# A fused attention and MLP kernel: in the first batch, each projection unit for the second batch computed in two halves, one in each of two steps, with Q's scale one step later and K's three

## The chip, the cores and the metric

The kernel runs on one core of one Trainium2 chip. The metric is the device time of one execution in microseconds (us). A run gives one such time; the profile below is of one more execution of the same program.

## What is computed

The input is 8 sequences of 1024 positions with 256 channels. An attention layer with 16 heads of 16 channels is followed by a layer norm, a three-layer MLP with weights of +1 and -1, and a second layer norm. The part of the reference that the change touches is the projection to q, k and v and what is done to it:

```python
qkv = (x @ w_qkv.T + b_qkv).reshape(b, n, 3, H, D).transpose(2, 0, 3, 1, 4)
q, k, v = (qkv[0], qkv[1], qkv[2])
q = jax.nn.elu(q) + 1.0
k = jax.nn.elu(k) + 1.0
q = _apply_rope(q, sin, cos)
k = _apply_rope(k, sin, cos)
attn = jnp.einsum('bhnd,bhmd->bhnm', q, k) * scale
attn = jax.nn.softmax(attn, axis=-1)
attn_out = jnp.einsum('bhnm,bhmd->bhnd', attn, v)
...
return attn_out + lepe
```

The MLP is `x @ w` three times with `relu(h) * 2` between, and each layer norm is taken over the sum of its input and the layer's result.

## The kernel before

**Steps.** A sequence is a batch, b. Its 16 heads are worked in 8 pairs (n counts pairs over all batches), and a pair in 8 steps, one for each tile kt of 128 keys: 64 steps a batch (`BATCH`), 512 in all. In step s, TensorE (PE) computes four "S" units, the scores of step s + 12 with queries on partitions, from which VectorE (DVE) takes a row maximum (`row_max`, L931), and four "T" units, the scores of step s with keys on partitions, on which ScalarE (ACT) takes the exponential (`exp_probs`, L763). S and T matmuls use different halves of the array and are issued in pairs (L559, L569). PE then multiplies the exponentials of step s - 1 with v (`weighted_v`, L604, "PV" below). A step's two halves are `scores_both(s, 0)` and `scores_both(s, 1)`.

**Units and the table.** All other matmul work is cut into units of one PSUM bank each, and a table written out by hand, `dealt()`, gives each a step. In batch 0 these are, for batch c = 1: four Q units and four K units ("proj", L631; two 128x512 float32 matmuls, one for each half of the 256 input channels, `kc`), four V units (L642, four 128x256 float32 matmuls), and two "scale" units (L587, L588) that sum the relu totals over heads. Two further kinds have fixed places: "O rows" (L619) in step kt = 2 and "max rows" (L612) in step kt = 5. In a step with dealt units PE's order is: `scores_both(s, 0)`, own units, dealt units, `scores_both(s, 1)`, then both halves of PV together. Without dealt units PV's first half stands between the two score blocks. `pieces_of` cuts a unit in two pieces, which the table puts into steps that follow each other; before, only MLP units L1 and L2 (from batch 1 on) are cut.

**Banks.** In batch 0 S units use banks 0, 1 and 4, T units banks 2 and 3, and all the others take banks 5 and 6 in turn. A unit takes its bank at its first piece (`wait_free`: the unit before it in this bank must have been read) and holds it until its reader is done.

**Readers.** In order, on ACT, step s does: two exponentials, the ELU of the Q or K unit whose last piece was the last dealt piece of step s - 1 (`elu_inputs`, L799 and L800), in kt = 2 the copy of O rows (L776), in some steps `copy_v` (L784), two exponentials, in kt = 0 `copy_o` (L769), and in steps 8 to 27 one piece of the MLP weights' conversion (`weights`, L831 or L835). DVE in step s does two row maxima, the V unit or scale of step s - 1 (`v_out`, L1012; `make_scale`), the max rows, `join_sums` (L967: it adds the relu totals, and the scale unit on PE waits for it by `sums_joined`), and two row maxima. GpSimd (POOL) takes the ELU's results on: `elu`, `rotate_side`, `split`, and a DMA to scratch in DRAM, from which SyncE's queue (SP) loads the stacks of pair 8 and later.

**Places in batch 0, before.** Q units in steps 6 to 9, `join_sums` for them in 11, their scale in 14; K units in 22 to 25, `join_sums` in 27, scale in 28; V units in 46 to 49. Later batches have their own table entries.

Of the kernel before, what the change touches and what calls it, by code (L numbers as in the profile page):

```python
# [34 lines left out]
NB, N, C = 8, 1024, 256  # L35
# [3 lines left out]
KC = C // P  # L39
# [25 lines left out]
O_ROWS_STEP, RECIPROCAL_STEP, MAX_ROWS_STEP = 2, 3, 5  # L65

Q_AT = 6
V_AT = {1: (46, 47, 48, 49)}
K_AT, SCALE_AT = {1: 22}, ({}, {1: 28})
STATS_AT = {**{6 + t // 2: (0, t) for t in range(0, T, 2)}, 27: (1, 4), 29: (1, 6), 59: (1, 0), 61: (1, 2)}  # L70
MOMENTS_AT = {10: 0, 31: 1}
NORMALISE_AT = ({13: 0, 14: 2, 15: 4, 16: 6}, {37 + t: t for t in range(T)})
# [4 lines left out]
def k_at(c):  # L77
    return K_AT.get(c, 32)


def v_at(c):
    return V_AT.get(c, (46, 51, 52, 53))

# [4 lines left out]

def pieces_of(unit):

    return [(unit, part) for part in range(2 if unit[0] in ("L1", "L2") else 1)]


def proj_units(c, which):
# [204 lines left out]
def build(nc, x, xT, wT, b_qk, b_v, w_lepe, b_lepe, cos, sin, k0, k1, k2, s0, s1, s2, out):  # L299
    with ExitStack() as ctx:  # L300
# [3 lines left out]
        def sem(name):  # L304
            return ctx.enter_context(nc.semaphore(name))
# [81 lines left out]
        w_kv_loaded = sem("w_kv_loaded")  # L387
# [6 lines left out]
        xT_loaded = sem("xT_loaded")  # L394
# [30 lines left out]
        units = Units(unit_banks, unit_full, unit_free)  # L425
# [127 lines left out]
        def _(pe):  # L553
# [26 lines left out]
            def head_bounds(unit):  # L580

                _, c, w = unit
                pe.wait_ge(dve_setup, 3)
                pe.wait_ge(sums_joined, 2 * c + w + 1)
                units.wait_free(pe, unit)
                bank, total = units.out(unit), sums[:, w:w + 1]
                nc.tensor.matmul(bank[:, 0:1], same_head[:], total, start=True, stop=True, skip_group_check=True)  # L587
                nc.tensor.matmul(bank[:, 1:1 + H], total.to_broadcast([P, P]), head_mask[:], start=True, stop=True,  # L588
                                 skip_group_check=True).then_inc(units.full_sem(unit), 1)
# [30 lines left out]
                                               o_sb[:, blk * P:(blk + 1) * P], ident[:])  # L620
                done.then_inc(units.full_sem(unit), 1)

            def project(unit):

                _, c, ct, half = unit
                pe.wait_ge(xT_loaded, (c + 1) * 16)
                if c == 0 and ct == 2 and half == 0:
                    pe.wait_ge(w_kv_loaded, 16)
                units.wait_free(pe, unit)
                for kc in range(KC):  # L630
                    done = nc.tensor.matmul(units.out(unit), wT_sb[:, kc, ct * P:(ct + 1) * P],  # L631
                                            xT_sb[:, kc, half * 512:(half + 1) * 512],
                                            start=kc == 0, stop=kc == KC - 1)
                done.then_inc(units.full_sem(unit), 1)

            def project_v(unit):
                _, c, i = unit
                units.wait_free(pe, unit)
                for t in range(2):
                    for kc in range(KC):  # L640
                        col = (2 * i + t) * P
                        done = nc.tensor.matmul(units.out(unit)[:, t * C:(t + 1) * C], xT_sb[:, kc, col:col + P],  # L642
                                                wT_sb[:, kc, 2 * C:3 * C], start=kc == 0, stop=kc == KC - 1)
                done.then_inc(units.full_sem(unit), 1)

            def transpose_h(unit):
                _, m, th, kc = unit
                if m == TAIL and th == 1:
                    pe.wait_ge(tail_done[0], T // 2)
                else:  # L650
                    pe.wait_ge(ln_done[0], m * T + T // 2 * (th + 1))
                units.wait_free(pe, unit)
                for t in range(4):
                    done = nc.tensor.transpose(units.out(unit)[:, t * P:(t + 1) * P],
                                               rows_of(m)[:, 4 * th + t, kc * P:(kc + 1) * P], ident[:])
                done.then_inc(units.full_sem(unit), 1)
# [35 lines left out]

            def dense(unit, part):
                if unit[0] == "proj":
                    project(unit)
                elif unit[0] == "V":
                    project_v(unit)
                elif unit[0] == "scale":
                    head_bounds(unit)
                elif unit[0] == "hT":  # L700
                    transpose_h(unit)
                elif unit[0] == "L2":
                    ffn_out(unit, part)
                else:
                    hidden(unit, part)
# [214 lines left out]
        def _(dve):  # L920
# [7 lines left out]
            def row_max(v, h, half):  # L928
                unit, t = ("S", v, h, half), v % T
                units.wait_full(dve, unit)  # L930
                nc.vector.reduce_max(maxima[:, v // T % 2, h * T + t, half:half + 1], units.out(unit), AXIS_X)\  # L931
                  .then_inc(units.free_sem(unit), 1)
# [185 lines left out]
            for s in range(STEPS):  # L1118
                n, kt = divmod(s, T)
                b, i = s // BATCH, s % BATCH  # L1120
                v = s + T + LEAD
                if v < STEPS:
                    for half in range(2):
                        row_max(v, 0, half)
                for unit in done_behind(s - 1):
                    dense(unit)
                for unit in own_units(s):
                    if unit[0] == "max rows":
                        split_max_rows(unit[1])
                for w, at in enumerate((Q_AT, k_at(b + 1))):  # L1130
                    if b + 1 < NB and i == at + 5:
                        join_sums(b + 1, w)
                if kt == RECIPROCAL_STEP and n > 0:
                    reciprocal_o(n - 1)
                for unit in done_within(s):
                    dense(unit)
                if i in STATS_AT:
                    which, t = STATS_AT[i]
                    m = b - 2 if which == 1 and t >= T // 2 else b - 1
                    if m >= 0:  # L1140
                        if which == 0 and t == 0:
                            dve.wait_ge(sum_ready, m + 1)
                        if which == 1:
                            units.wait_read(dve, ("L2", m, t // (T // 2), t % (T // 2) // 2))
                        for tile in (t, t + 1):
                            ln_stats_of(m, which, tile)
                if i in MOMENTS_AT:
                    which = MOMENTS_AT[i]
                    m = b - 1 - which
                    if m >= 0:  # L1150
                        ln_moments(m, which)
                if v < STEPS:
                    for half in range(2):
                        row_max(v, 1, half)
                    if v % T == T - 1:
                        join_maxima(v // T)
# [37 lines left out]
            for unit in END_UNITS[len(LATE_UNITS):]:  # L1194
# [6 lines left out]
                if unit[:3] == ("L2", m, 1):  # L1201
                    t = T // 2 + 2 * unit[3]
# [208 lines left out]
```

## Time and profile before

| | |
|---|---|
| median of 3 runs | 2185.26 us |
| the 3 runs | 2184.11, 2188.7, 2185.26 us |
| profiled execution, its own time | 2188.8 us |
| its span | 2187.0 us |
| mean granted TensorE clock | 0.982 of full |
| PE busy | 2104.7 us, 96% of the span |
| DVE busy | 1673.0 us, 76% |
| ACT busy | 1491.6 us, 68% |
| POOL busy | 916.1 us, 42% |

Busy time of PE is rough, since ends of matmuls are modelled: the starts of its instructions tell more than its busy share. Batch 0 runs from step 0 at 86.80 us to step 64 at 286.77 us of the span. Steps are found in the trace by counting ACT's exponentials (L763), four a step; a step's time below is that of its first exponential. Step 6 begins at 105.71 us, step 16 at 141.26, step 22 at 159.18, step 32 at 195.22, step 46 at 232.81, step 55 at 262.13. The time from the first exponential of a step to that of the next, before, is:

| steps | us each |
|---|---|
| 6 to 15 | 4.26, 3.99, 4.87, 3.85, 4.33, 2.92, 2.90, 2.75, 2.91, 2.78 |
| 22 to 31 | 3.85, 3.99, 4.54, 3.66, 4.14, 3.07, 4.77, 2.81, 2.73, 2.48 |
| 46 to 54 | 4.27, 4.00, 4.17, 3.83, 2.80, 2.49, 2.48, 2.69, 2.58 |

### The profile page before, as it was taken

How to read it: one execution, taken by the hardware profiler on the slowest of the kernel's cores; microseconds unless marked ns; L12 is line 12 of the kernel's file. 1: busy time of each engine (PE TensorE's matmuls, PEld its weight loads, DVE VectorE, ACT ScalarE, POOL GpSimd, SP SyncE). 2: the span in 40 equal slices, each digit the busy share in tenths (PEclk: the TensorE clock that was granted, in tenths of full speed). 3: DMA queues.
4: the chain of work that ended last, by engine and by line, in shares of the span. 5: the costliest groups of instructions: out<-in, count | busy, mean ns of one | idle time of the engine just before them, and what ended most of it. 6: DMA issues, size and time to landing. Idle time of an engine off the chain costs nothing.

```text
span 2187.0 us, 43073 instructions
## 1 busy us (share of the span) xinstructions
PE 2104.7 (96%) x16896; PEld 850.9 (39%) x16896; DVE 1673.0 (76%) x3027; ACT 1491.6 (68%) x2867; POOL 916.1 (42%) x530
## 2 busy tenths in 40 slices
PE   4999999999999999999999999999999999999988
PEld 2133333344433434334343443434343343434345
DVE  7888888787787887778787877878778788877233
ACT  3298788766767667776777767776677766767532
POOL 2548159430856037470484407661275704300000
PEclk8599999999999999999999999999999999999999
DMA  5101110011010200111000110002101110000001
GB/s 179 31 14 41 54 37 26 25 49 38 16 35 18 87 17 9 35 55 54 14 25 25 66 40 16 28 16 75 31 15 35 31 56 16 16 9 28 2 0 39
DMA packets 40428, 76.85 MB, mean 35 GB/s; under 512 B 15025, under 2 KB 19489, under 8 KB 37281
## 3 DMA queue, kind: packets, MB, share of 16 engines
q1 hardware_dynamic: 35040, 51.02, 8.5%
q0 software_dynamic: 5184, 23.07, 2.8%
q8 instruction: 134, 2.20, 0.4%
q14 instruction: 70, 0.57, 0.1%
HBM read 46.27 MB, written 25.17 MB: 33 GB/s over the span
## 4 chain that ended last, share of the span: by engine, by line
PE 83%; DVE 10%; ACT 4%; issue 1%; DMA 1%; SPq 0%; POOL 0%; POOLq 0%; DVEq 0%; ACTq 0%
PE unit_banks L674 25%; PE unit_banks L559 22%; PE o_bank L604 20%; DVE maxima L931 6%; PE unit_banks L687 5%; PE unit_banks L631 5%; ACT probs L763 3%; PE unit_banks L642 2%; PE unit_banks L569 2%; PE unit_banks L619 1%; DVE hT L1000 1%; DVE h0T L1003 1%; PE unit_banks L612 0%; ACT h0T L822 0%; DMA xT_sb<-in_xT 0%
## 5 line engine op out<-in xcount | busy, mean ns | idle before, releaser
L931 DVE TENSOR_REDUCE maxima<-unit_banks 128x1 f32<-128x512 f32 x2048 | 1308.2, 684 | 367.9 <-PE unit_banks L559 364.1
L763 ACT ACTIVATE probs<-unit_banks 128x512 f32<-128x512 f32 x2048 | 1115.9, 597 | 565.6 <-PE unit_banks L569 559.9
L559 PE MATMUL unit_banks<-k_stack,q_stack 48*128 48x512 f16 x2048 | 655.1, 391 | 44.1 <-DMA k_stack<-k_scratch 23.4
L569 PE MATMUL unit_banks<-q_stack,k_stack 50*128 50x512 f16 x2048 | 648.9, 386 | 4.7 <-ACT probs L763 3.5
L604 PE MATMUL o_bank<-probs,v_pair 128*32 128x256 f32 x8192 | 565.5, 388 | 0.6
L674 PE MATMUL unit_banks<-h0T,w 128*128 128x512 f16 x2048 | 480.2, 380 | 0.0
L1258 POOL TENSOR_TENSOR attn<-o_rows_sb,rden 128x256 f32<-128x256 f32 x63 | 39.2, 622 | 875.8 <-DVE rden L944 864.7
L559 PEld LDWEIGHTS unit_banks<-k_stack,q_stack 48*128 48x128 f16 x2048 | 154.8, 94 | 562.8 <-DVE maxima L931 277.1
L604 PEld LDWEIGHTS o_bank<-probs,v_pair 128*32 128x32 f32 x8192 | 207.4, 109 | 297.6 <-issue 217.9
L674 PEld LDWEIGHTS unit_banks<-h0T,w 128*128 128x128 f16 x2048 | 188.9, 98 | 223.9 <-issue 34.2
L569 PEld LDWEIGHTS unit_banks<-q_stack,k_stack 50*128 50x128 f16 x2048 | 155.2, 93 | 36.2 <-ACT probs L763 27.7
L1003 DVE SCALAR_TENSOR_TENSOR h1T<-unit_banks,h1T 128x512 f16<-128x512 f32 x128 | 87.3, 682 | 79.9 <-ACT h1T L822 79.8
L1274 POOL TENSOR_TENSOR lepe_tmp<-v_ext,lepe_rows 128x1024 f32<-128x1024 f32 x48 | 113.1, 2357 | 70.3 <-DVE max_rows L952 67.7
L631 PE MATMUL unit_banks<-xT_sb,wT_sb 128*128 128x512 f32 x256 | 126.5, 622 | 9.8 <-DMA xT_sb<-in_xT 9.8
L674 PE MATMUL unit_banks<-hT,w 128*128 128x512 f16 x512 | 124.4, 386 | 3.5 <-DVE hT L1000 2.2
L687 PE MATMUL unit_banks<-w,h1T 128*128 128x256 f16 x1024 | 123.2, 275 | 2.7 <-DVE h1T L1003 2.7
L1276 POOL TENSOR_TENSOR rows<-rows,lepe_tmp 128x1024 f32<-128x1024 f32 x48 | 113.2, 2359 | 3.8
L822 ACT ACTIVATE h1T<-unit_banks 128x512 f16<-128x512 f32 x128 | 77.1, 602 | 49.3 <-PE unit_banks L674 49.3
L1290 POOL TENSOR_TENSOR neg_mean<-moments,ln_consts 128x8 f32<-128x8 f32 (+2 forms) x18 | 3.8, 210 | 251.7 <-DVE moments L1042 251.7
L687 PEld LDWEIGHTS unit_banks<-w,h1T 128*128 128x128 f16 x1024 | 97.2, 99 | 25.4 <-issue 10.4
L1003 DVE SCALAR_TENSOR_TENSOR h0T<-unit_banks,h0T 128x512 f16<-128x512 f32 x128 | 87.6, 686 | 18.7 <-ACT h0T L822 18.5
L822 ACT ACTIVATE h0T<-unit_banks 128x512 f16<-128x512 f32 x128 | 77.5, 605 | 16.3 <-PE unit_banks L674 13.1
(126 smaller groups left out, 1556.7 us busy)
## 6 DMA issues: line engine op xcount, KB each, us to landing
rows<-in_x POOLq DMA_DIRECT2D x8, 1024.0 KB, 5.2
xT_sb<-in_xT SPq DMA_DIRECT2D x8, 1024.0 KB, 14.2
q_stack<-q_scratch SPq DMA_DIRECT2D x128, 64.0 KB, 2.1
k_stack<-k_scratch SPq DMA_DIRECT2D x128, 64.0 KB, 2.0
q_scratch<-parts POOLq DMA_DIRECT2D x14, 512.0 KB, 3.3
k_scratch<-parts POOLq DMA_DIRECT2D x14, 512.0 KB, 3.3
out<-rows SPq DMA_DIRECT2D x7, 1024.0 KB, 4.0
q_stack<-q_scratch SPq DMA_DIRECT2D x128, 32.0 KB, 1.9
```

What stands on the lines that cost most here:

```text
L559: nc.tensor.matmul(units.out(unit), q_stack[row:row + STACK, r, t * P:(t + 1) * P], k_stack[row:row + STACK, r, half * 512:(half + 1) * 51 ...
L569: nc.tensor.matmul(units.out(unit), k_stack[row:end, r, kt * P:(kt + 1) * P], q_stack[row:end, r, half * 512:(half + 1) * 512], start=True ...
L604: done = nc.tensor.matmul(o, v_pair[:, n % RING, kt, h, :], p[:, :, parity, :], start=kt == 0 and half == 0, stop=kt == T - 1, skip_group_ ...
L631: done = nc.tensor.matmul(units.out(unit), wT_sb[:, kc, ct * P:(ct + 1) * P], xT_sb[:, kc, half * 512:(half + 1) * 512], start=kc == 0, st ...
L674: done = nc.tensor.matmul(units.out(unit), w, a, start=k == 0 and i == 0, stop=k == tiles - 1 and i == 1)
L687: done = nc.tensor.matmul(units.out(unit)[:, t * C:(t + 1) * C], h1T[:, a, k, (2 * i + t) * P:(2 * i + t + 1) * P], w2[:, k, :], start=k = ...
L763: nc.scalar.activation(probs[:, 2 * (kt % 2) + h, half * 512:(half + 1) * 512], units.out(unit), ACT.Exp, scale=exp_regs[2 * (n % PAIRS) + ...
L822: done = nc.scalar.activation(dst[:, 0, unit[3], :], units.out(unit), ACT.Relu)
L931: nc.vector.reduce_max(maxima[:, v // T % 2, h * T + t, half:half + 1], units.out(unit), AXIS_X)\
L1003: free(unit, nc.vector.scalar_tensor_tensor(dst[:, 1, u, :], s, 0.0, dst[:, 0, u, :], ALU.max, ALU.subtract))
L1274: ins = combine(lepe_tmp[:], v_ext[:, t + tap:t + tap + T // 2, :], row(tap), ALU.mult)
L1276: ins = combine(base, base, lepe_tmp[:], ALU.add)
```

## The change

In batch 0 every Q, K and V unit for batch 1 is cut in two pieces. A Q or K unit does the first half of the input channels in one step and the second in the next; a V unit does one of its two tiles in each. The number of matmuls is the same. Q units now stand in steps 6 to 13, K units in 22 to 29, V units in 46 to 53. The scale of Q moves from step 14 to 15, that of K from 28 to 31. `join_sums` of batch 0 moves from 4 steps back of these places to the same steps, 15 and 31. The other batches' entries are as they were.

```diff
-V_AT = {1: (46, 47, 48, 49)}
-K_AT, SCALE_AT = {1: 22}, ({}, {1: 28})
+V_AT = {1: (46, 48, 50, 52)}
+K_AT, SCALE_AT = {1: 22}, ({1: 15}, {1: 31})
...
-    return [(unit, part) for part in range(2 if unit[0] in ("L1", "L2") else 1)]
+    halved = unit[0] in ("L1", "L2") or unit[0] in ("proj", "V") and unit[1] == 1
+    return [(unit, part) for part in range(2 if halved else 1)]
...
-            def project(unit):
+            def project(unit, part):
...
-                for kc in range(KC):
+                for kc in range(KC) if pieces == 1 else (part,):
                     done = nc.tensor.matmul(units.out(unit), wT_sb[:, kc, ct * P:(ct + 1) * P],
                                             xT_sb[:, kc, half * 512:(half + 1) * 512],
                                             start=kc == 0, stop=kc == KC - 1)
-                done.then_inc(units.full_sem(unit), 1)
...
+                if part == pieces - 1:
+                    done.then_inc(units.full_sem(unit), 1)
...
-                for t in range(2):
+                for t in range(2) if pieces == 1 else (part,):
...
-                    if b + 1 < NB and i == at + 5:
+                    if b + 1 < NB and i == at + (9 if b == 0 else 5):
                         join_sums(b + 1, w)
```

On PE, step 10 stood like this before: two pairs of scores, the four transposes of O rows (L619), PV's first half, two pairs of scores, PV's second half.

```order
L559 MATMUL unit_banks<-k_stack,q_stack 128x512
L569 MATMUL unit_banks<-q_stack,k_stack 128x512
L559 MATMUL unit_banks<-k_stack,q_stack 128x512
L569 MATMUL unit_banks<-q_stack,k_stack 128x512
L619 MATMUL unit_banks<-ident,o_sb 128x128 x4
L604 MATMUL o_bank<-probs,v_pair 32x256 x4
L559 MATMUL unit_banks<-k_stack,q_stack 128x512
L569 MATMUL unit_banks<-q_stack,k_stack 128x512
L559 MATMUL unit_banks<-k_stack,q_stack 128x512
L569 MATMUL unit_banks<-q_stack,k_stack 128x512
L604 MATMUL o_bank<-probs,v_pair 32x256 x4
```

In the changed kernel (L560, L570, L605, L620 and L634 are L559, L569, L604, L619 and L631 of before) the same step reads:

```order
L560 MATMUL unit_banks<-k_stack,q_stack 128x512
L570 MATMUL unit_banks<-q_stack,k_stack 128x512
L560 MATMUL unit_banks<-k_stack,q_stack 128x512
L570 MATMUL unit_banks<-q_stack,k_stack 128x512
L620 MATMUL unit_banks<-ident,o_sb 128x128 x4
L634 MATMUL unit_banks<-xT_sb,wT_sb 128x512
L560 MATMUL unit_banks<-k_stack,q_stack 128x512
L570 MATMUL unit_banks<-q_stack,k_stack 128x512
L560 MATMUL unit_banks<-k_stack,q_stack 128x512
L570 MATMUL unit_banks<-q_stack,k_stack 128x512
L605 MATMUL o_bank<-probs,v_pair 32x256 x8
```

The first piece of the third Q unit (L634) now stands behind O rows, and PV has moved to the step's end in one block. O rows takes bank 5 and the Q unit bank 6; bank 6 was held by the second Q unit, whose last piece is in step 9. K's third unit stands the same way in step 26 (its bank: 5, held by the second K unit), and V's third unit in step 50 (bank 6, held by the second V unit).

On ACT, from step 8 to the O rows of step 10, the changed kernel has these rows (L770 the exponentials, L806 and L807 the ELU of a Q unit, L776 `copy_o`, L838 a weight piece, L783 the O rows):

```order
L806 ACTIVATE work<-unit_banks,bias_qk 128x512
L807 ACTIVATE work,relu_sum<-unit_banks,bias_qk 128x512
L770 ACTIVATE probs<-unit_banks 128x512 x2
L776 ACTIVATE o_sb<-o_bank 128x512
L838 ACTIVATE w<-rows,s_work 128x512
L770 ACTIVATE probs<-unit_banks 128x512 x4
L838 ACTIVATE w<-rows,s_work 128x512
L770 ACTIVATE probs<-unit_banks 128x512 x2
L806 ACTIVATE work<-unit_banks,bias_qk 128x512
L807 ACTIVATE work,relu_sum<-unit_banks,bias_qk 128x512
L783 ACTIVATE o_rows_sb<-unit_banks 128x512
```

The ELU that reads bank 6 (the second pair of L806 and L807) is in step 10 too, behind that step's first two exponentials. Before, an ELU stood in each of the steps 7 to 10; now one stands in each of 8, 10, 12 and 14.

## Rows read from the trace of the kernel before

**Rows 1.** The page: busy time, share of the span and instructions.

```profile
PE 2104.7 (96%) x16896; PEld 850.9 (39%) x16896; DVE 1673.0 (76%) x3027; ACT 1491.6 (68%) x2867; POOL 916.1 (42%) x530
```

**Rows 2.** Windows: stretch, length, busy PE, PEld, DVE, ACT, POOL, clock, DMA, GB/s.

```profile
105.71:141.26 35.55, 34.14 (x271) 11.57 (x275) 26.90 (x49) 32.56 (x64) 18.79 (x9) 1.00 0.05 11
159.18:195.22 36.04, 34.94 (x265) 11.41 (x264) 26.21 (x49) 30.74 (x63) 31.90 (x18) 0.91 0.16 47
181.00:187.80 6.80, 6.80 (x42) 2.19 (x42) 4.12 (x9) 4.12 (x9) 6.39 (x5) 0.51 0.22 81
232.81:262.13 29.32, 29.22 (x255) 12.77 (x255) 25.49 (x45) 20.52 (x39) 1.16 (x2) 1.00 0.17 51
```

**Rows 3.** PE's timeline, step 6 and start of 7: start us, us, what, [idle before].

```profile
106.06 1.98 PE L631 MATMUL unit_banks<-xT_sb,wT_sb 128*128 128x512 f32 x4
107.97 0.39 PE L559 MATMUL unit_banks<-k_stack,q_stack 48*128 48x512 f16 x1
...
108.51 1.07 PE L604 MATMUL o_bank<-probs,v_pair 128*32 128x256 f32 x16
109.51 0.39 PE L559 MATMUL unit_banks<-k_stack,q_stack 48*128 48x512 f16 x1
```

**Rows 4.** PE's timeline: PV alone, next scores, O rows, scale.

```profile
207.76 0.64 PE L604 MATMUL o_bank<-probs,v_pair 128*32 128x256 f32 x8
208.33 0.39 PE L559 MATMUL unit_banks<-k_stack,q_stack 48*128 48x512 f16 x1
...
122.50 0.66 PE L619 MATMUL unit_banks<-ident,o_sb 128*128 128x128 f32 x4
123.08 0.64 PE L604 MATMUL o_bank<-probs,v_pair 128*32 128x256 f32 x8
...
135.37 0.38 PE L587 MATMUL unit_banks<-sums,same_head 128*128 128x1 f32 x2
...
135.92 0.39 PE L559 MATMUL unit_banks<-k_stack,q_stack 48*128 48x512 f16 x1
```

**Rows 5.** ACT's timeline, first exponential of step 7, steps 9, 10, 13.

```profile
109.97 1.08 ACT L763 ACTIVATE probs<-unit_banks 128x512 f32<-128x512 f32 x2 [0.45 <-PE unit_banks L569]
...
118.83 1.07 ACT L763 ACTIVATE probs<-unit_banks 128x512 f32<-128x512 f32 x2
119.78 0.70 ACT L799 ACTIVATE work<-unit_banks,bias_qk 128x512 f32<-128x512 f32 x1
...
121.02 1.11 ACT L763 ACTIVATE probs<-unit_banks 128x512 f32<-128x512 f32 x2
...
122.68 1.12 ACT L763 ACTIVATE probs<-unit_banks 128x512 f32<-128x512 f32 x2
...
132.82 2.15 ACT L763 ACTIVATE probs<-unit_banks 128x512 f32<-128x512 f32 x4
...
135.57 2.15 ACT L763 ACTIVATE probs<-unit_banks 128x512 f32<-128x512 f32 x4
```

**Rows 6.** ACT's timeline, first exponentials of steps 27, 28 and 29.

```profile
179.36 1.19 ACT L763 ACTIVATE probs<-unit_banks 128x512 f32<-128x512 f32 x2
...
182.43 1.08 ACT L763 ACTIVATE probs<-unit_banks 128x512 f32<-128x512 f32 x2
...
187.20 1.09 ACT L763 ACTIVATE probs<-unit_banks 128x512 f32<-128x512 f32 x2 [1.75 <-PE unit_banks L569]
```

**Rows 7.** DVE's timeline: a V unit's copy, then four row maxima.

```profile
250.26 0.68 DVE L1012 TENSOR_TENSOR v_ext<-unit_banks,lepe_rows 128x512 f32<-128x512 f32 x1
250.85 2.47 DVE L931 TENSOR_REDUCE maxima<-unit_banks 128x1 f32<-128x512 f32 x4
```

**Rows 8.** POOL's timeline: second half of K's ELU.

```profile
189.79 2.77 POOL L1230 TENSOR_SCALAR h1T<-h1T 128x1024 f32<-128x1024 f32 x1
```

**Rows 9.** SP's timeline: first stack load of batch 1, edges of v.

```profile
234.88 0.37 SPq L464 DMA_DIRECT2D q_stack<-q_scratch  x1
...
265.38 0.64 SPq L482 DMA_DIRECT2D v_ext<-v_ext  x1
```

More of the change, by code:

```diff
@@ L621, in o_rows @@
                 done.then_inc(units.full_sem(unit), 1)
-            def project(unit):
+            def project(unit, part):
                 _, c, ct, half = unit
[L626 to L629, printed above, removed]
-                for kc in range(KC):
+                pieces = len(pieces_of(unit))
+                if part == 0:
+                    pe.wait_ge(xT_loaded, (c + 1) * 16)
+                    if c == 0 and ct == 2 and half == 0:
+                        pe.wait_ge(w_kv_loaded, 16)
+                    units.wait_free(pe, unit)
+                for kc in range(KC) if pieces == 1 else (part,):
                     done = nc.tensor.matmul(units.out(unit), wT_sb[:, kc, ct * P:(ct + 1) * P],
@@ L633, in project, with project_v @@
                                             start=kc == 0, stop=kc == KC - 1)
-                done.then_inc(units.full_sem(unit), 1)
-            def project_v(unit):
+                if part == pieces - 1:
+                    done.then_inc(units.full_sem(unit), 1)
+            def project_v(unit, part):
                 _, c, i = unit
-                units.wait_free(pe, unit)
-                for t in range(2):
+                pieces = len(pieces_of(unit))
+                if part == 0:
+                    units.wait_free(pe, unit)
+                for t in range(2) if pieces == 1 else (part,):
                     for kc in range(KC):
@@ L643, in project_v @@
                                                 wT_sb[:, kc, 2 * C:3 * C], start=kc == 0, stop=kc == KC - 1)
-                done.then_inc(units.full_sem(unit), 1)
+                if part == pieces - 1:
+                    done.then_inc(units.full_sem(unit), 1)
             def transpose_h(unit):
@@ L694, in dense @@
                 if unit[0] == "proj":
-                    project(unit)
+                    project(unit, part)
                 elif unit[0] == "V":
-                    project_v(unit)
+                    project_v(unit, part)
                 elif unit[0] == "scale":
```

## The prediction

> **What bounds the kernel now.** The page first: PE is busy for 96% of the span [rows 1], DVE and ACT for 76% and 68%. That is an average, and the change touches only batch 0, so the timelines of its three stretches count. After batch 0 nothing is moved, and no other engine has a queue that could swallow a shift, so what batch 0 loses or gains I carry to the end in full.
>
> PE's starts give the price of a step's parts. A whole Q unit takes 1.91 us from its start to the next scores (106.06 to 107.97), a block of two score pairs 0.54, both halves of PV together 1.00 (108.51 to 109.51) [rows 3]. PV's half alone takes 0.57, O rows 0.58, a scale 0.55 [rows 4]. So a step without a dealt unit needs 2 x 0.54 + 2 x 0.57 = 2.22 us of PE, a step with one 0.54 + 1.91 + 0.54 + 1.00 = 3.99, and the table of steps shows 3.99 for step 7. DVE needs 2.47 for its four maxima [rows 7]. Where nothing is dealt (step 51: 2.49) DVE sets the step and PE has about a quarter of a us to spare.
>
> ACT's rows show the third bound. Two exponentials take 0.95, an ELU 1.24 (119.78 to 121.02), a weight piece 0.71 (the 1.66 up to 122.68 less 0.95) [rows 5]. A step with weights alone is 2.75 (132.82 to 135.57) [rows 5], one with an ELU too 0.95 + 1.24 + 0.95 + 0.71 = 3.85, as step 9 shows. In steps 8 to 27, where the weights are converted, ACT is the bound in most steps: it is busy for 32.56 of the 35.55 us of steps 6 to 15 [rows 2]. In steps 46 to 49 PE is the bound: 29.22 busy of 29.32 [rows 2].
>
> **The change, part by part. Splitting.** A half unit costs PE half of the unit plus a second entry. The entry's price I read from PV: twice 0.57 less 1.00 is 0.14 saved when two groups of matmuls are one [rows 3, 4]. So a half is (1.91 - 0.14) / 2 + 0.14 = 1.03, and a step with a half 0.54 + 1.03 + 0.54 + 1.00 = 3.11. The bounds: 0.885 if a cut costs nothing beyond the unit's own entry (0.14 of it once), 1.11 if it costs twice as much as PV's. I take 1.03, since PV is the nearest row of the same float32 kind.
>
> The Trainium skill (TensorE: Matmul & The Clock Gate, Part 2: What happens when you issue a matmul) says that one matmul's drain overlaps the next one's fill, so back-to-back matmuls are spaced by their columns alone. By that a half is 0.955, and with some 18 halves on PE's path the sum would be 1.3 us lower. No row here shows a cut unit of this kind; PV's 0.14 speaks for more.
>
> What it would bring if nothing else moved: a whole unit and a free step are 3.99 + 2.49 = 6.48, two halves 6.22. That is 0.26 a unit, about 3 us for twelve.
>
> **The bank wait.** It is not free. With two banks for all these units and each unit holding its bank over two steps, the third Q unit (step 10), the third K unit (26) and the third V unit (50) begin in the very step in which the reader empties their bank. In step 10 PE issues scores and O rows, and then waits for ACT's ELU, which is behind two exponentials; behind PE's wait are the next scores, for which ACT itself waits. From ACT's first exponential: 0.95 + 1.24 until the bank is read, 0.1 for the signal, 1.03 for the half unit, 0.45 from a T matmul to its exponential (109.51 to 109.97) [rows 3, 5], 0.95 and 0.71: 5.4 us for step 10, against 4.33 before. PE stands for about 1.6 us of it (0.45 + 0.95 + 1.24 + 0.1 less the scores' 0.54 and O rows' 0.58). In step 26 the sum is 5.45 with weights of 0.5, against 4.14. In step 50 the wait is for DVE: 0.43 to the first maximum, half of 2.47, 0.59 for V's copy (250.26 to 250.85) [rows 7], 0.1, then 1.03 + 0.54 + 1.00 on PE: 4.95 against 2.80.
>
> **The scales.** `join_sums` now stands in the scale's own step. DVE reaches it only after the two maxima of scores that PE has just issued, so PE stands for about 0.6 us before L587 in steps 15 and 31, and ACT's second pair of exponentials comes 0.5 to 0.8 late.
>
> **The sum, step by step** (times as in the table of steps; where ACT bounds, its rows; where PE does, 3.11; ACT's order moves the ELUs to 8, 10, 12, 14 and 24, 26, 28, 30).
> Steps 6 to 15: 4.26 - 0.88 = 3.38, then 3.11, 4.34, 2.8, 5.4, 3.1, 3.85, 3.2, 3.85, 3.1: 36.1, against 35.55 [rows 2]. **+0.6.**
> Steps 22 to 31: 3.0, 3.1, 4.15, 2.7, 5.45, 3.1, 3.5, 3.4, 3.35, 3.4: 35.15 against 36.04 [rows 2]. **-0.9.** But this stretch of before holds 6.8 us at half the granted clock, 0.51 from 181.00 to 187.80 [rows 2], and steps 27 and 28 took 7.84 us (179.36 to 187.20) [rows 6], where 2.9 and 2.75 would be ACT's need. With the step behind them that is about 2.5 us, and without it this term is +1.6.
> Steps 46 to 54: 3.4, 3.11, 3.3, 2.95, 4.95, 3.11, 3.11, 3.3, and 54 with V's last copy 2.6 + 0.6 less DVE's earlier lag: 30.0 against 29.32 [rows 2]. **+0.7.**
> Together +0.4 against the profiled execution's 2188.8: 2189.2. That execution is 3.5 us above the median 2185.26, and the other two low runs fit one without the slow clock in step 27. Against the median I therefore add 2.5 + 0.4 = 2.9: 2188.2. Small terms (max rows, the scale's work on DVE in other steps) may add a few tenths: I say **2188.5**.
>
> **What is late next, and hidden.** K's last ELU moves from step 26 to 30, about 190 us. POOL begins the second half of it at 189.79 [rows 8], so its chain shifts by at most 2 us, and the stacks it feeds are loaded at 234.88 [rows 9] for scores of step 52, at some 254. The edges of v are sent at 265.38 [rows 9], behind a load that V's last copy at 262 doesn't hold up. Both cost nothing; if the cover were gone, each us late would be one of the span.
>
> **The rivals.** *B, the clock falls in the new stalls.* PE's granted clock fell at 181 after a step with some 0.8 us of idle, and halved PE's rate for 6.8 us at a price of 2.5 [rows 2, 6]. The new waits of 1.6 us in steps 10 and 26 are twice as long. Against it: step 10 had 1.03 us of idle in before and no drop. One drop more gives 2190.9, two 2193.5.
> The skill's same page (A second HAM failure mode: psum-queue depth-cycling) says that idling between matmul groups while cycling through PSUM banks makes the clock swing; by that the drops come, and the trace has one such swing in this batch.
>
> *C, the averaging wins.* If a half costs only 0.885, a step with one is 2.965, and the gain is 6.48 - 5.93 = 0.55 a unit, 6.6 us for twelve; with the waits in 10, 26 and 50 costing half of what I reckon because ACT and DVE arrive earlier there, 2180 is reached. It decides from a half below 0.95 and waits below 0.8 us. For it: PE-bound steps of 3.99 next to DVE-bound ones of 2.49. Against: ACT bounds steps 8 to 27, and its work stays the same.
>
> *D, nothing.* The shares cancel and the time stays at 2185.3 plus or minus 1: PE's total work is the same but for entries.
>
> **How the numbers follow.** My forecast (a loss of 1 to 5 us) 0.50, with a range of its own of 2186 to 2190.5; B 0.24; C 0.14; D 0.12. The range 2183 to 2193 leaves out the second drop and the larger half of C. Within 0.2%, 4.4 us, a measurement of this kernel can't tell a difference: that is 2180.9 to 2189.6. Faster is half of C: 0.08. Slower is B with the upper end of mine: 0.33. Same 0.59.
>
> **What would show it.** PE idle of about 1.6 us behind L620 in steps 10 and 26, ended by ACT's ELU, and about 1.2 us in step 50, ended by DVE's V copy; steps of 5.4, 5.45 and 4.95 there. PE's half unit at 1.03 from its start to the next scores, and steps of 3.11 in 46 to 53. A wait of PE for DVE's `join_sums` before both scales. ELUs on ACT in 8, 10, 12, 14. Wrong it would be if those waits are a few tenths, if the clock is at half for more of batch 0, or if a later batch changes its length.

## The result and the profile after

The changed kernel takes 2190.81 us (median of 21 runs, 2188.27 to 2194.61), the kernel before 2186.83 us (median of 21 runs, 2183.93 to 2191.16). The ratio is 1.0015, with a 95% interval of 1.0008 to 1.0021: a loss of 1.7 to 4.6 us, clear of the noise, though but for its upper end it lies inside the 0.2% that I called no change. The forecast was 2188.5, in a range of 2183 to 2193, some 3 us above the median then known (2185.26, of 3 runs). The medians now differ by 4.0 us, the ratio of 1.0015 stands for 3.3.

The page of the changed kernel says no more than that of before [rows 1]:

```profile
span 2190.1 us, 43072 instructions
PE 2103.4 (96%) x16896; PEld 849.2 (39%) x16896; DVE 1674.6 (76%) x3027; ACT 1491.0 (68%) x2867; POOL 915.9 (42%) x530
```

The windows of its three stretches answer to [rows 2]; columns are the stretch, its length, busy PE, PEld, DVE, ACT and POOL, the granted clock, the DMA share and GB/s. The first is steps 6 to 15, the third 22 to 31, the last 46 to 54.

```profile
105.69:143.26 37.57, 34.56 (x267) 11.30 (x267) 27.05 (x47) 32.55 (x63) 18.80 (x9) 0.96 0.05 12
140.30:143.70 3.40, 3.40 (x26) 0.87 (x28) 1.76 (x3) 2.23 (x4) 2.47 (x2) 0.51 0.04 12
161.55:198.49 36.94, 34.03 (x265) 10.87 (x264) 26.50 (x46) 30.65 (x62) 30.79 (x17) 0.95 0.17 51
177.80:181.20 3.40, 3.40 (x22) 0.73 (x20) 1.29 (x2) 1.60 (x3) 2.01 (x2) 0.50 0.20 77
236.16:265.60 29.44, 28.20 (x253) 12.07 (x251) 25.58 (x45) 20.52 (x38) 1.16 (x2) 1.00 0.17 51
```

The work is the same (ACT 32.55 us in the first stretch against 32.56), but the stretch is longer. And two stretches at half the granted clock, of 3.4 us each, stand in this part of the trace, where before had one of 6.8. PE's waits from 105 to 266 us name the new idle time; columns are who waits for whom, us in all, times, longest:

```profile
PE unit_banks L570 <- ACT probs L770: 2.0, 6, 0.5
PE unit_banks L634 <- ACT h1T L807: 1.7, 1, 1.7
PE unit_banks L634 <- ACT work L807: 1.7, 1, 1.7
PE unit_banks L648 <- DVE v_ext L1019: 1.2, 1, 1.2
PE unit_banks L588 <- issue: 0.9, 2, 0.4
```

Before had only 2.7 us for ACT's exponentials here and 0.2 for DVE. The three new waits are those of the third Q, K and V unit for their bank. PE's timeline of step 10, and ACT's beside it, show the chain that I reckoned:

```profile
119.60 0.66 PE L620 MATMUL unit_banks<-ident,o_sb 128*128 128x128 f32 x4
122.00 1.10 PE L634 MATMUL unit_banks<-xT_sb,wT_sb 128*128 128x512 f32 x2 [1.74 <-ACT work L807]
123.03 0.39 PE L560 MATMUL unit_banks<-k_stack,q_stack 48*128 48x512 f16 x1
```

```profile
119.53 1.08 ACT L770 ACTIVATE probs<-unit_banks 128x512 f32<-128x512 f32 x2
120.50 0.69 ACT L806 ACTIVATE work<-unit_banks,bias_qk 128x512 f32<-128x512 f32 x1
121.06 0.70 ACT L807 ACTIVATE work<-unit_banks,bias_qk 128x512 f32<-128x512 f32 x1
...
121.73 0.61 ACT L783 ACTIVATE o_rows_sb<-unit_banks 128x512 f32<-128x512 f32 x1
123.48 1.08 ACT L770 ACTIVATE probs<-unit_banks 128x512 f32<-128x512 f32 x2 [1.14 <-PE unit_banks L570]
```

Two exponentials (119.53), the ELU (120.50 to 121.73), then the half unit at 122.00, 1.03 us long to the next scores, and the next exponentials 0.45 us behind those: PE stands for 1.74 us and ACT for 1.14. The same wait in steps 26 and 50:

```profile
177.31 1.56 PE L634 MATMUL unit_banks<-xT_sb,wT_sb 128*128 128x512 f32 x2 [1.74 <-ACT h1T L807]
250.63 1.13 PE L648 MATMUL unit_banks<-wT_sb,xT_sb 128*128 128x256 f32 x4 [1.17 <-DVE v_ext L1019]
```

Counting the exponentials gives each step of each trace. Steps repeat within a few hundredths of a us from trace to trace wherever the clock is full and their program is the same, so steps are a far finer measure here than whole runs. This table is worked out from them, in us; "clean" takes each step from a trace of the same program in which the clock was full there. Before, steps 27 to 31 are from the run with V spaced (label v_gap), whose Q and K steps are those of before. In the changed kernel, steps 15, 16 and 26 are from its second trace (label again), all others from its first; for steps 46 to 54, where both traces have the full clock, both are given.

| steps | before, its trace | before, clean | changed, its trace | changed, clean | clean difference |
|---|---|---|---|---|---|
| 6 to 15 | 35.55 | 35.55 | 37.57 | 36.32 | +0.8 |
| 16 to 21 | 17.92 | 17.92 | 18.29 | 18.02 | +0.1 |
| 22 to 31 | 36.04 | 34.0 | 36.94 | 35.36 | +1.4 |
| 32 to 45 | 37.59 | 37.59 | 37.67 | 37.67 | +0.1 |
| 46 to 54 | 29.32 | 29.32 | 29.44 | 29.44, 29.64 | +0.1 to +0.3 |
| 55 to 63 | 24.64 | 24.64 | 24.72 | 24.72 | +0.1 |

At full clock the change costs 2.6 us (2.5 to 2.7 by the row of steps 46 to 54), all in batch 0. From step 64 to 448 the two traces run apart by 0.34 us in 1531. The start up to step 6 (105.71 and 105.69 us in these two, 103.3 to 104.2 in most others) and the end from step 511 on (118.93 and 118.11, and 114.7 to 119.0 over all) together differ between traces by more than the change does, and this is most of the 7 us over which whole runs spread.

### The profile page after: what moved, and what is told of

Its sections match the earlier page's. It is cut to its first block, busy times and chain, and to the rows that moved or that the text cites. A ratio compares the mean times of both kernels' runs of the same rounds, so it can differ in the third digit from the quotient of the medians.

```text
span 2190.1 us, 43072 instructions
## 1 busy us (share of the span) xinstructions
PE 2103.4 (96%) x16896; PEld 849.2 (39%) x16896; DVE 1674.6 (76%) x3027; ACT 1491.0 (68%) x2867; POOL 915.9 (42%) x530
## 3 DMA queue, kind: packets, MB, share of 16 engines
q8 instruction: 133, 2.18, 0.4%
## 4 chain that ended last, share of the span: by engine, by line
PE 84%; DVE 10%; ACT 4%; issue 1%; DMA 1%; SPq 0%; POOL 0%; POOLq 0%; DVEq 0%; ACTq 0%
PE unit_banks L681 25%; PE unit_banks L560 22%; PE o_bank L605 20%; DVE maxima L938 6%; PE unit_banks L694 5%; PE unit_banks L634 5%; ACT probs L770 3%; PE unit_banks L648 2%; PE unit_banks L570 2%; PE unit_banks L620 1%; DVE hT L1007 1%; DVE h0T L1010 1%; PE unit_banks L613 0%; ACT h0T L829 0%; DVE stats L1043 0%
## 5 line engine op out<-in xcount | busy, mean ns | idle before, releaser
L770 ACT ACTIVATE probs<-unit_banks 128x512 f32<-128x512 f32 x2048 | 1115.2, 597 | 570.4 <-PE unit_banks L570 565.4
L560 PE MATMUL unit_banks<-k_stack,q_stack 48*128 48x512 f16 x2048 | 654.4, 391 | 43.9 <-DMA k_stack<-k_scratch 23.4
L570 PE MATMUL unit_banks<-q_stack,k_stack 50*128 50x512 f16 x2048 | 647.7, 386 | 4.0 <-ACT probs L770 2.8
L605 PE MATMUL o_bank<-probs,v_pair 128*32 128x256 f32 x8192 | 563.4, 388 | 0.6
L560 PEld LDWEIGHTS unit_banks<-k_stack,q_stack 48*128 48x128 f16 x2048 | 153.9, 94 | 563.9 <-DVE maxima L938 277.8
L605 PEld LDWEIGHTS o_bank<-probs,v_pair 128*32 128x32 f32 x8192 | 208.8, 109 | 299.0 <-issue 217.8
L570 PEld LDWEIGHTS unit_banks<-q_stack,k_stack 50*128 50x128 f16 x2048 | 154.8, 93 | 35.4 <-ACT probs L770 27.3
L634 PE MATMUL unit_banks<-xT_sb,wT_sb 128*128 128x512 f32 x256 | 128.9, 626 | 13.2 <-DMA xT_sb<-in_xT 9.7
```

What stands on the lines that cost most here:

```text
L560: nc.tensor.matmul(units.out(unit), q_stack[row:row + STACK, r, t * P:(t + 1) * P], k_stack[row:row + STACK, r, half * 512:(half + 1) * 51 ...
L570: nc.tensor.matmul(units.out(unit), k_stack[row:end, r, kt * P:(kt + 1) * P], q_stack[row:end, r, half * 512:(half + 1) * 512], start=True ...
L605: done = nc.tensor.matmul(o, v_pair[:, n % RING, kt, h, :], p[:, :, parity, :], start=kt == 0 and half == 0, stop=kt == T - 1, skip_group_ ...
L770: nc.scalar.activation(probs[:, 2 * (kt % 2) + h, half * 512:(half + 1) * 512], units.out(unit), ACT.Exp, scale=exp_regs[2 * (n % PAIRS) + ...
```

## The experiments

Beside the runs of each kernel below, the kernel before was run again, and the second time and the ratio refer to that. Steps are read from one trace of each kernel. First, V alone halved, and then V alone halved with step 50 left free. Against the changed kernel:

```diff
-    halved = unit[0] in ("L1", "L2") or unit[0] in ("proj", "V") and unit[1] == 1
+    halved = unit[0] in ("L1", "L2") or unit[0] == "V" and unit[1] == 1
-K_AT, SCALE_AT = {1: 22}, ({1: 15}, {1: 31})
+K_AT, SCALE_AT = {1: 22}, ({}, {1: 28})
-                    if b + 1 < NB and i == at + (9 if b == 0 else 5):
+                    if b + 1 < NB and i == at + 5:
```

and for the second also

```diff
-V_AT = {1: (46, 48, 50, 52)}
+V_AT = {1: (46, 48, 51, 53)}
```

> Only the V units are halved (steps 46 to 53); Q, K, their sums and scales stand as before. Bank-wait theory (the third unit of each group waits for its bank, and that eats what the halving gives): steps 46 to 54 take 29.4 us as in the changed kernel (29.32 before), with step 50 at 4.95 and an idle of 1.2 us on PE in it; the rest is as before, so the time is within 0.3 us of before in an undisturbed comparison. Rival (the halving itself costs, by the entries of the halves, wherever it is done): steps 46 to 49 and 51 to 53 show no gain over 3.99 and 2.49 in turn, and the time is 1 us or more above before.

> As the run with V alone halved, but the third and fourth V unit start in steps 51 and 53, so that step 50, with O rows, has no piece and no unit meets a bank that its reader frees in the same step. Bank-wait theory: no idle of PE for V's copy; step 50 takes 2.8 us, the eight steps with a half 3.1 to 3.3 each; steps 46 to 63 take 52.9 us (53.96 before, 54.16 changed), and the time is 1.1 us below before. Rival (halving costs): steps 46 to 63 at 54.2 or more.

V alone halved: 2186.68 us against 2187.55 (ratio 0.9993, 0.9983 to 1.0002). Steps 46 to 54 took 29.70 us, those of before 29.32; step 50 took 4.97. The steps read 3.41, 3.14, 3.31, 2.97, 4.97, 3.14, 3.14, 3.15, 2.49. The first pairs take 6.55 and 6.28 us, where a whole unit's step and a free one took 4.27 + 2.49 and 4.17 + 2.49; step 50 takes it back. The bank-wait theory held for step 50 (4.97 us, 4.95 expected) and against its rival, since the pairs do gain; the stretch itself came out 0.3 us longer than the 29.4 expected. The whole runs can't tell 0.3 us from nothing.

With step 50 free I was wrong: 2190.19 us against 2187.55 (1.0013, 1.0003 to 1.0022). Step 50 fell to 2.80 as expected, but step 53 rose to 4.97, and steps 46 to 63 took 55.0 us and not 52.9. (That run's slow clock in steps 11 to 18 and beyond batch 0 is in its time too.) PE's timeline of step 53:

```profile
256.53 1.13 PE L648 MATMUL unit_banks<-wT_sb,xT_sb 128*128 128x256 f32 x4 [1.55 <-DVE v_ext L1019]
257.59 0.39 PE L560 MATMUL unit_banks<-k_stack,q_stack 48*128 48x512 f16 x1
```

I had overlooked the max rows of step 53, which take bank 5 ahead of V's fourth unit, so that this one meets the bank of the third, whose last piece is in step 52. The wait moved with the conflict, and the step that has it takes 4.97 us again.

Next, two edits of the changed kernel. In the first the scales stand one step behind the sums:

```diff
-K_AT, SCALE_AT = {1: 22}, ({1: 15}, {1: 31})
+K_AT, SCALE_AT = {1: 22}, ({1: 16}, {1: 32})
```

In the second all twelve units skip the step with O rows, as V did above, and the sums and scales come later:

```diff
-V_AT = {1: (46, 48, 50, 52)}
-K_AT, SCALE_AT = {1: 22}, ({1: 15}, {1: 31})
+V_AT = {1: (46, 48, 51, 53)}
+K_AT, SCALE_AT = {1: 22}, ({1: 17}, {1: 33})
...
-        deal(b + Q_AT, proj_units(c, 0))
+        for half in range(2):
+            deal(b + Q_AT + half * (5 if c == 1 else 2), proj_units(c, 0)[2 * half:2 * half + 2])
... (K in the same way)
-                    if b + 1 < NB and i == at + (9 if b == 0 else 5):
+                    if b + 1 < NB and i == at + (10 if b == 0 else 5):
```

> The changed kernel with the scales one step behind the sums (16 and 32 in place of 15 and 31). Theory that the sum in the scale's own step costs: the 0.44 us of PE idle ahead of each scale goes, steps 15 and 16 lose 0.5 to 1 us together, steps 31 and 32 too, if the clock is the same; the waits of 1.74 us in steps 10 and 26 stay. Rival (ACT bounds there, so the wait is hidden): steps 6 to 21 and 22 to 31 within 0.2 us of the changed kernel's but for the clock.

> All twelve units are halved, but the third unit of each group starts one step later (Q in 6 to 9 and 11 to 14, K in 22 to 25 and 27 to 30, V in 46 to 49 and 51 to 54), the sums are joined in 16 and 32 and the scales stand in 17 and 33. Bank-wait theory: no wait of PE for ACT's ELU or DVE's V copy; step 10 takes 4.33 and step 26 4.14 as before; steps 6 to 15 about 35.2 (35.55 before, 37.57 changed), 22 to 31 about 33.7 (36.04 with a stretch at half clock before, 36.94 changed), 46 to 63 about 52.9. No drop of the clock in batch 0. The time is 2 to 4 us below before and about 6 below the changed kernel. Rival (the halving itself costs): within 1 us of the changed kernel. Rival (the clock alone): steps as in the changed kernel where the clock is full, the waits remaining.

Scales later: 2184.93 us against 2187.55 (0.9997, 0.9987 to 1.0007). Its trace has the full clock from step 6 to the end of batch 0. Steps 15 and 16 took 2.81 + 3.78 against 3.00 + 3.66 clean, steps 31 and 32 2.52 + 3.09 against 3.41 + 2.98. So the sum in the scale's own step costs 0.1 us at Q, where ACT bounds, and 0.8 at K: the theory held for the one and its rival for the other. Steps 10 and 26 stayed at 5.64 and 5.50. The whole runs gained more on the changed kernel than these 0.9 us (ratios 0.9997 and 1.0015), and their mean granted clock was higher: 0.983 to 0.986 in the ten runs, 0.981 to 0.984 in the 21 of the changed kernel. Why it was higher no run shows.

All units with a free step: 2193.27 us against 2187.55 (1.0022, 1.0013 to 1.0031), the opposite of the 2 to 4 us below before that I expected, for the reason seen above. Steps 10 and 26 fell to 4.34 and 4.15, as expected, and steps 13, 29 and 53, with the max rows, rose to 5.63, 7.08 (at half clock) and 4.97. PE's timeline of step 13:

```profile
127.98 0.28 PE L615 MATMUL unit_banks<-ident,max_both 128*16 128x128 f32 x1
130.51 1.10 PE L636 MATMUL unit_banks<-xT_sb,wT_sb 128*128 128x512 f32 x2 [2.25 <-ACT work L809]
```

The third placement then counts both own units. Q starts at 6, 8, 11 and 14, K at 22, 24, 27 and 30, V at 46, 48, 51 and 54:

```diff
-        deal(b + Q_AT, proj_units(c, 0))
+        for u, unit in enumerate(proj_units(c, 0)):
+            deal(b + Q_AT + ((0, 2, 5, 8)[u] if c == 1 else u), [unit])
... (K in the same way)
-V_AT = {1: (46, 48, 50, 52)}
-K_AT, SCALE_AT = {1: 22}, ({1: 15}, {1: 31})
+V_AT = {1: (46, 48, 51, 54)}
+K_AT, SCALE_AT = {1: 22}, ({1: 18}, {1: 34})
...
-                    if b + 1 < NB and i == at + (9 if b == 0 else 5):
+                    if b + 1 < NB and i == at + (11 if b == 0 else 5):
```

> All twelve units halved, each starting two steps or more behind the end of the piece that held its bank (Q at 6, 8, 11, 14; K at 22, 24, 27, 30; V at 46, 48, 51, 54; sums in 17 and 33, scales in 18 and 34), so no unit meets a bank that is freed in its own step. Bank-wait theory: PE has no wait for ELU or V copy anywhere; steps 10, 26 and 50 at 4.34, 4.15 and 2.80, and no step of 5.6 or 5.0 in batch 0; steps 6 to 21 take 53.8 us (53.47 before, 54.29 in the run with the scales later), 46 to 63 some 54.2 (53.96 before). That means the halving itself brings nothing: over the batch 0 to 2 us above a run of before without a stretch at half clock. Rival (without the waits the halving brings its 0.26 us a unit): 3 us below before, steps 46 to 63 at 53.0 or less.

It took 2188.3 us against 2187.3 (0.9997, 0.9987 to 1.0007). No wait for an ELU or a V copy is left; PE's waits from 103 to 290 us are these two kinds:

```profile
PE unit_banks L572 <- ACT probs L772: 4.8, 8, 1.1
PE unit_banks L562 <- DVE maxima L940: 2.7, 6, 0.8
```

Steps 6 to 15 took 34.50 (35.55 before), 22 to 31 33.52 (34.0 clean), 46 to 54 28.56 (29.32), but 32 to 45 took 38.70 (37.59) and 55 to 63 25.11 (24.64). Steps 17 to 19 stood at half clock and can't be read. So the three groups save 2.3 us, and steps 16, 32 to 45 and 55 to 63 give back 2.4 (step 16 took 4.33 against 3.55). Steps 46 to 63 took 53.67 us, 0.3 below before: between the 54.2 of the theory and the 53.0 of its rival, so neither had it right. The steps that grew are those to which units, readers and scales have moved; which engine sets each of them wasn't tested.

Is it the bank, or the place of the units? Two more kernels give batch 0's other units three banks and the S units two, the kernel before and the changed one, with no unit moved:

```diff
-    rings = {"S": (0, 1, 4), "T": (2, 3), "": (5, 6, 4, 0, 1, 2, 3)}
+    rings = {"S": (0, 1), "T": (2, 3), "": (5, 6, 4, 0, 1, 2, 3)}
-    rings[""] = (5, 6)
+    rings[""] = (5, 6, 4)
```

> The kernel before with the three banks 5, 6 and 4 in turn for all units but scores in batch 0, and two (0, 1) in place of three for the S units, as the later batches have it. Base for the next run. Nothing waited for a unit's bank in batch 0, so nothing is gained there; with one bank less DVE's row maxima have less lead, and steps with extra work on DVE (kt 3, 4 and 5) grow by up to 0.3 us each: 0 to 5 us over batch 0.

> The changed kernel with the same three banks. Bank-wait theory: the third unit of each group now takes a bank freed two steps earlier, PE has no wait for ELU or V copy; step 10 takes 4.33, step 26 4.15, step 50 3.6 us, and steps 6 to 15, 22 to 31 and 46 to 54 fall by 1.3 us each against the changed kernel at full clock, so that batch 0 is within 1 us of the same base with whole units. Rival (the units' placement on ACT and DVE, not the bank, costs): step 10 over 5 us as before this edit, and the difference to the base stays near 2.6.

Base: 2200.0 us against 2186.74 (1.0055, 1.0035 to 1.0075); changed: 2197.23 (1.0047, 1.0030 to 1.0064), four runs each, too few to tell the two apart by whole runs. The base lost more than the 0 to 5 us expected: steps 22 to 63, clean, lost 6.0, and I had not counted the scores ahead of step 0 (which begins at 91.38 and 92.25 us against 86.80). In the changed one PE's waits from 103 to 290 us hold none for an ELU or a V copy:

```profile
PE unit_banks L560 <- DVE maxima L938: 6.4, 23, 0.7
PE unit_banks L588 <- issue: 0.9, 2, 0.4
PE unit_banks L570 <- ACT probs L770: 0.6, 2, 0.4
```

In step 10 the unit follows O rows without a pause:

```profile
124.77 0.66 PE L620 MATMUL unit_banks<-ident,o_sb 128*128 128x128 f32 x4
125.26 1.02 PE L634 MATMUL unit_banks<-xT_sb,wT_sb 128*128 128x512 f32 x2
```

Steps 10, 26 and 50 took 4.34, 4.16 and 3.55, expected 4.33, 4.15 and 3.6. On this base the halving wins: steps 22 to 30, at full clock in both, 31.02 against 32.64, and steps 46 to 54 29.32 against 30.52. Even step 31 with its late sum (3.41 clean) leaves 0.9 us in K and there are 1.2 in V. The bank waits are 1.30, 1.34 and 1.42 us by the difference of these steps to 5.64, 5.50 and 4.97. Together that is 4.1 us, and with the 0.9 of the late sums 5.0, where the change as a whole costs 2.6 at full clock: by this estimate the halving itself saves 2.4 us, not far from the 3 forecast, and the bank waits alone turn that into a loss. The base matters a little. In steps 46 to 54 the two S banks cost both kernels some 1.2 us (the bank wait left aside), but in steps 22 to 31 they cost whole units 1.3 us and halved ones 0.4, so up to 0.9 us of the gain in K may be this base's. Against the changed kernel with its own banks the stretches fell by 1.3 us (Q), 0.9 (K) and 0.1 to 0.3 (V), where I expected 1.3 each.

Who sets a step with a wait? In steps 10, 26 and 50 of the changed kernel, PV goes ahead of the waiting unit:

```diff
+                pv_first = s in (10, 26, 50)
+                if pv_first:
+                    weighted_v(s - 1, 0)
+                    weighted_v(s - 1, 1)
                 for unit, part in DEALT[s]:
                     dense(unit, part)
```

> The changed kernel, but in steps 10, 26 and 50 both halves of PV stand ahead of the unit that waits for its bank. Theory that ACT sets steps 10 and 26 and PE sets 50: PE's idle ahead of the unit falls from 1.74, 1.74 and 1.17 to about 0.75, 0.75 and 0.17 us, but steps 10 and 26 stay at 5.4 to 5.6 (but for the clock), while step 50 falls from 4.96 to 4.0. Rival (PE's idle is lost one for one): steps 10 and 26 fall by 1.0 too.

One run, 2187.6 us. PE's waits from 103 to 290 us:

```profile
PE unit_banks L634 <- ACT h1T L811: 0.7, 1, 0.7
PE unit_banks L634 <- ACT work L811: 0.7, 1, 0.7
PE unit_banks L648 <- DVE v_ext L1023: 0.2, 1, 0.2
```

A microsecond of PE's idle time is gone from each, and steps 10 and 26 take 5.64 and 5.45 (5.64 and 5.50 without the edit): ACT's order sets them. Step 50 fell by 0.47, half of what I expected, and step 51 rose by 0.30. DVE's four maxima run without a pause there (2.48 us from 250.01), so DVE may be what comes next, but no run tests it.

The join by itself, in the kernel before:

```diff
-                    if b + 1 < NB and i == at + 5:
+                    if b + 1 < NB and i == at + ((8, 6)[w] if b == 0 else 5):
```

> The kernel before with one edit: the sums are joined in the scale's own step (14 and 28) in place of 11 and 27; nothing is halved. Theory: PE idles about 0.44 us ahead of each scale, and DVE 1.05 us behind each join; steps 14 and 15 take 0.3 to 0.8 us more than 2.91 + 2.78, and steps 28 and 29 0.5 to 1.0 more than the 5.5 us of a run of before at full clock. Rival: ACT and the banks hide it, no change over 0.1 us.

One run, 2190.16 us. Steps 14 and 15 took 3.94 + 2.76 against 2.91 + 2.78, and PE stood for 1.41 us ahead of the scale:

```profile
134.38 0.35 PE L587 MATMUL unit_banks<-sums,same_head 128*128 128x1 f32 x2 [1.41 <-issue]
```

That is 1.0 us, of which step 16 gives back 0.1, and more than expected: the wait is 1.41 us where it is 0.44 in the changed kernel's step 15. I take it that DVE is further behind PE there; that isn't shown. Steps 27 to 30 stood at half clock, so its price at K can't be read.

The changed kernel once more:

> The changed kernel once more. Theory that the stretches at half clock fall at places that vary from run to run: they stand elsewhere than at 140.3 and 177.8 us or are missing, and where they are missing steps 15 and 16 take 3.3 and 3.4 and step 26 takes 5.45. Rival (the new waits bring them): they stand again behind steps 10 to 15 and in step 26.

One run, 2189.45 us. The stretches at half clock stood elsewhere: not at 140.3, and in step 10 and steps 31 and 32 in place of step 26. Windows of this trace:

```profile
120.30:123.70 3.40, 3.40 (x22) 0.72 (x20) 1.29 (x2) 1.78 (x3) 0.00 (x0) 0.50 0.02 5
191.90:198.80 6.90, 6.67 (x46) 2.46 (x48) 3.21 (x10) 2.59 (x5) 6.66 (x4) 0.51 0.10 26
```

Steps 15 and 16 took 3.00 and 3.66, step 26 5.50: near the 3.3, 3.4 and 5.45 expected. Step 10, which then ran at half clock behind its wait, took 7.08, 1.44 more than at full clock. The theory held for steps 15, 16 and 26, but a drop behind the wait in step 10 is what its rival named.

Last, the two kernels with ACT relieved in the Q and K steps:

```diff
-WEIGHTS_AT = 8
+WEIGHTS_AT = 28
```

> The kernel before with the conversion of the MLP weights on ACT in steps 28 to 47 in place of 8 to 27, so that ACT is not the bound in the Q and K steps. Reckoned from the rows: steps 6 to 15 in 32.8 us (35.55 before), as PE's 3.99 sets 7 to 9. The later steps without a dealt unit grow to 2.75. It is the base for the next run; the whole is within 3 us of before.

> The changed kernel with the weights' conversion in steps 28 to 47. Bank-wait theory: ACT's 0.71 goes from steps 8 to 27, the waits stay (step 10 at 4.93, step 26 at 4.9 where the clock is full), steps 6 to 15 take 33.6 us, still 0.8 above the same base. Rival (ACT's load hides the gain of halving, and without the weights it appears): steps 6 to 15 take 32 us or less, below the base, in spite of the wait.

With this edit the kernel before took 2183.82 us against 2187.66 (0.9988, 0.9978 to 0.9998), the fastest of all here; the changed kernel took 2195.95 (1.0031, 1.0013 to 1.0048). The times of the changed kernel lie in two groups: four runs of 2186.2 to 2187.5 us at a mean granted clock of 0.985, among them the profiled one, and six of 2194.9 to 2200.3 at 0.979 or 0.980. No trace shows the second group, so only the steps are compared. Both traces have the full clock from step 6 to the end of batch 0. Steps 6 to 15: 33.11 and 35.36. The difference is 2.25 us, not 0.8: step 10 is 5.50, hardly below the 5.64 with the weights, because with ACT's 0.71 gone PE's own 0.54 and 1.00 behind the half unit set its end, and step 13 with its piece and step 15 with the scale and its late sum took 3.45 and 3.41 against 2.69 and 2.48. From step 6 to 64 the two are 4.5 us apart, against 2.6 with the weights where they were. ACT's load was thus hiding a loss, not a gain.

## Why the prediction was right

**The mechanism** was the one on record. The three bank waits stood where I put them: steps 10, 26 and 50 took 5.64, 5.50 and 4.97 at full clock, where I had 5.4, 5.45 and 4.95, and PE idled for 1.74, 1.74 and 1.17 us, where I had 1.6, 1.6 and 1.2. The kernel with a third bank shows them to be the bank's and worth 1.3 to 1.4 us each. Two readings of before were off, without weight in the sum: PE's idle time near step 10 is 0.93 us and not 1.03, and 29.22 busy of 29.32 is that of steps 46 to 54, not of the PE-bound 46 to 49 alone.

**The half unit** measured 1.03 us to the next scores (122.00 to 123.03), as taken from PV's two forms; a V half 1.06. PE-bound steps with a half were 3.13 to 3.15 (3.11). The Trainium skill's rule for back-to-back matmuls (TensorE: Matmul & The Clock Gate, Part 2: What happens when you issue a matmul), from which I had estimated 0.955, isn't what a cut unit costs between other kinds of matmuls: the measured 1.03 decides.

**The sum.** Q: +0.6 forecast, +0.8 clean (36.1 against 36.32). K: 35.15 forecast, 35.36 clean; +1.6 against a before at full clock, measured +1.4, since I had the slow clock's price in before as 2.5 and it was 2.0 (36.04 less 34.0). V: +0.7 forecast, +0.1 to +0.3 measured: step 54 took 2.49 and not 2.8, so V's last copy did not make DVE late, and steps 46 and 53 took 0.05 to 0.25 less than reckoned. Together 2.9 forecast and 2.6 measured at full clock; errors of both signs stand in it. **The scales**: 0.6 us of idle forecast, 0.44 measured; together worth 0.9 us.

**The level** owes something to luck. I put the median of 2185.26 down to runs without the slow clock in step 27. But the profiled execution was long for three reasons: 2.0 us in steps 27 to 31, steps 0 to 5 at 18.9 us where seven of the fourteen traces have 17.4, and an end from step 511 on of 118.93, where nine have 114.7 to 116.5. With 21 runs the median of before is 2186.83. Against 2188.5 the measured 2190.81 is 2.3 higher, of which 1.6 is this base.

**The clock**, rival B, is not settled for single steps. A wait of 1.7 us or more for a bank stands twice in each of five traces (the changed kernel, its repetition, the free steps, the later scales, the later weights). In three of these ten places the granted clock fell 0.5 or 0.6 us behind the wait's end (177.31 and 177.8 us in the changed kernel, 119.68 and 120.3 in its repetition, 186.48 and 187.0 with the free steps), and that added 1.6 us to the step in the first and 1.4 in the second; for the third there is no step at full clock to compare. In the other seven it did not. And it fell in kernels with no such wait: at 181 us in before, at 126 with V spaced, for 10.2 us in the kernel without any bank wait. What the Trainium skill says of clock swings while cycling through PSUM banks (TensorE: Matmul & The Clock Gate, A second HAM failure mode) fits the three and not the others. The whole runs say more, since each has its mean granted clock: it is 0.9829 over 22 runs of the changed kernel and 0.9827 over 76 of before, taken beside the experiments. So there is no sign that the change lowers the clock of whole runs. Runs with the same clock differ as follows, on the mean: at 0.982, 2191.4 us (10 runs) against 2187.9 (24), and at 0.984, 2189.1 (9) against 2186.2 (16). That is 2.9 to 3.5 us, where the steps in batch 0 show 2.6; the rest, and the 4.0 of the medians, lie within the spread of the runs.

**Rival C**, that the averaging wins, failed on its conditions: the half was 1.03 and not 0.95, the waits 1.2 to 1.7 and not 0.8. Without the waits there is a gain, but on the base with three banks it is 0.9 us in K and 1.2 in V, and with the waits moved away whole runs equal before (0.9997): nothing like C's 6.6 us. **POOL** was late as reckoned (its ELU's second half began at 194.28, waiting 2.18 us, against 189.79 [rows 8]): 4.5 us later, of which 2.4 is the later start of step 22. Steps 46 to 63 took their usual time, so no score of the next batch waited for it.

## What to carry to other kernels

A unit cut over two steps holds its bank one step longer, from its first piece until its reader is done. Before spreading work over more steps, list for each bank who holds it and when its reader is done, own units of fixed steps included: I missed one such unit myself, and the wait only moved. A piece that starts in the step in which its bank is emptied costs the reader's whole chain, and what it costs is read on the engine that sets that step, not on the one that idles.

## What the runs showed of the hardware that was not expected

Steps repeat within a few hundredths of a us over all fourteen traces where their program is the same and the clock is full (steps 192 to 255: 257.74 to 257.85 us), while steps 0 to 5 took 16.3 to 19.1 us and the time from step 511 to the end 114.7 to 119.0. Both follow the granted clock. In every trace it is at half from some point between 36.6 and 39.5 us until one between 92.8 and 102.2, although TensorE is 97% busy from 58 to 75 us in before. The stretch ends in step 1, 2 or 3. Where this stretch lasted 54.6 us, steps 0 to 5 took 16.3 to 16.6 us, with 58.0 they took 17.4, and with 61.4 or 64.9, 18.5 to 19.1. The end took 114.7 us with no stretch at half clock in it but the one with which every trace closes, 116.4 or 116.5 with one of 3.4 us, 118.1 with two, and 118.9 or 119.0 with one of 3.4 and one of 6.8.

The granted clock fell between steps 6 and 64 in eleven of the fourteen, for 3.4, 6.8, 10.2 or 13.7 us, at places that changed from trace to trace, also between two of the same program. But the sixteen falls begin in eight steps only: four in step 17, three each in 27 and 31, two in 11 and one each in 10, 15, 26 and 29, and none in steps 32 to 63, though PE waits there for a V copy for 1.2 to 1.6 us in seven traces. The three in step 31 are all of kernels that join K's sum in that step. In the three traces without a fall (later scales, and both with the later weights) nothing else sets them apart that I can name, and no run shows a cause.
